# Four graph layers on one core: own features by a crossbar DMA, the last columns of v by matmuls, and the first chunk's adjacency rows loaded early

## The reference, cut to what matters

```python
h = relu(layernorm(x)); x = x + leaky_relu(A_norm @ [h[:2048] @ Wr; h[2048:] @ Wd] + bias)      # layer 0
h = relu(layernorm(x))                                                                          # layers 1 and 2
g = relu(concat([h, adj @ h], 1) @ W1);  x = x + relu(concat([g, adj @ g], 1) @ W2)
h = relu(layernorm(x)); x = x + relu((A_norm @ h) @ W.T + b)                                     # layer 3
h = relu(layernorm(x))                                                                          # attention
Wh1, Wh2 = (h @ W) @ a[:256], (h @ W) @ a[256:]
e = leaky_relu(Wh1 + Wh2.T, 0.2)
att, natt = softmax(where(adj > 0, e, -inf)), -softmax(where(adj > 0, -e, -inf))
x = x + elu(concat([att @ h, natt @ h], 1) @ wtrans)
```

## Time and profile before

| | us |
|---|---|
| median of 3 runs | 2246.96 (2246.89 to 2247.9) |
| the profiled execution, its own time | 2249.18 |
| its span, from the first to the last instruction | 2247.4 |
| PE busy | 2110.6 (94%) |
| ACT busy | 1473.8 (66%) |
| DVE busy | 1422.0 (63%) |
| mean granted TensorE clock | 0.98 of full |

### The profile page before, as it was taken

One profiled execution on the slowest core, in us unless ns is written; L12 is line 12 of the kernel. 1 busy time (PEld: TensorE's weight loads), 2 busy tenths in 40 slices (PEclk: granted clock), 3 DMA queues, 4 the chain that ended last, 5 costly groups with the idle time before them and its releaser, 6 DMA issues.

```text
span 2247.4 us, 27564 instructions
## 1 busy us (share of the span) xinstructions
PE 2110.6 (94%) x10932; PEld 1533.1 (68%) x10932; DVE 1422.0 (63%) x2335; ACT 1473.8 (66%) x1778; POOL 2.1 (0%) x12
## 2 busy tenths in 40 slices
PE   2678999999999999999998879999999999999998
PEld 2557888455554555554555358888888888888886
DVE  5667488100004332324445589999999999999774
ACT  5556666555547656556654457869686969787963
POOL 0000000000000000000000000000000000000000
PEclk9889999999999999999998989999999999999999
DMA  9989325100021101231117754626262627271300
GB/s 306 296 296 310 110 85 169 47 20 19 10 85 38 57 29 57 66 101 57 49 37 158 240 185 148 225 94 218 95 212 86 233 77 242 76 243 57 113 19 10
DMA packets 157647, 279.40 MB, mean 124 GB/s; under 512 B 10960, under 2 KB 83408, under 8 KB 149200
## 3 DMA queue, kind: packets, MB, share of 16 engines
q1 hardware_dynamic: 149072, 269.27, 36.5%
q10 hardware_dynamic: 8448, 8.39, 1.2%
HBM read 244.06 MB, written 33.57 MB: 124 GB/s over the span
## 4 chain that ended last, share of the span: by engine, by line
PE 81%; DVE 8%; DMA 6%; ACT 3%; issue 2%; SPq 0%; DVEq 0%; POOL 0%; ACTq 0%
PE ps L1604 39%; PE ps L1496 29%; PE ps L1521 6%; DMA work<-in_adj_t 5%; PE ps L1371 3%; ACT big L510 1%; PE ps L1467 1%; PE ps L1437 1%; DVE feat L1194 1%; PE ps L1424 1%; DMA t_spill<-acc 1%; DVE feat L1198 1%; DVE stat L1131 1%; DVE work L1130 1%; DVE work L1126 1%
## 5 line engine op out<-in xcount | busy, mean ns | idle before, releaser
L1496 PE MATMUL ps<-work,feat 128*128 128x512 bf16 x3072 | 671.3, 380 | 6.1 <-DVE feat L1068 4.3
L510 ACT ACTIVATE work<-big 128x1024 bf16<-128x1024 uint8 x460 | 481.4, 1053 | 244.3 <-PE ps L1496 222.0
L1496 PEld LDWEIGHTS ps<-work,feat 128*128 128x128 f16 x3072 | 300.1, 98 | 364.0 <-issue 6.8
L1604 PE MATMUL ps<-big,work 128*128 128x257 f32 x2048 | 452.0, 381 | 4.8 <-ACT work L808 4.8
L1604 PE MATMUL ps<-big 128*128 128x257 f32 x2048 | 449.4, 380 | 2.7 <-ACT big L808 2.7
L1604 PEld LDWEIGHTS ps<-big,work 128*128 128x128 f32 x2048 | 389.2, 191 | 61.0 <-issue 5.6
L1604 PEld LDWEIGHTS ps<-big 128*128 128x128 f32 x2048 | 388.3, 190 | 58.8 <-ACT big L808 3.5
L1371 PE MATMUL ps<-feat,work 128*128 128x256 f16 x2048 | 242.6, 280 | 13.7 <-DVE work L1002 7.1
L1371 PEld LDWEIGHTS ps<-feat,work 128*128 128x128 bf16 x2048 | 203.4, 100 | 51.0 <-DVE work L1002 11.7
L1100 DVE TENSOR_REDUCE gmax<-work 128x1 f32<-128x256 f32 x32 | 11.8, 414 | 261.9 <-ACT work L644 261.9
L808 ACT ACTIVATE work<-work 128x2048 f32<-128x2048 f32 x64 | 122.2, 1909 | 82.9 <-DVE work L1294 82.9
(11 more groups left out here) (158 smaller groups left out, 1562.4 us busy)
## 6 DMA issues: line engine op xcount, KB each, us to landing
work<-in_adj_t SPq DMA_DIRECT2D x128, 512.0 KB, 5.0
big<-in_adj_t SPq DMA_DIRECT2D x64, 1024.0 KB, 5.4
feat<-in_adj SPq DMA_DIRECT2D x58, 1024.0 KB, 7.3
h_spill<-work SPq DMA_DIRECT2D x32, 512.0 KB, 4.4
feat<-h_spill SPq DMA_DIRECT2D x32, 512.0 KB, 5.4
x_spill<-work SPq DMA_DIRECT2D x24, 512.0 KB, 3.0
work<-in_x SPq DMA_DIRECT2D x16, 512.0 KB, 5.5
work<-x_spill SPq DMA_DIRECT2D x16, 512.0 KB, 4.2
```

The lines of the kernel that those rows point to most:

```text
L510: return nc.scalar.activation(out_, in_, ACT.Copy, **kw)
L1496: ins = mm(ps[:, bank + f, :], parts[:, j, h, f * P:(f + 1) * P], stage[:, g % STAGES, jj, :], start=(fresh and h == 0), stop=(end and h = ...
L1604: ins = mm(ps[:, 4 * s + t, 0:YW], quads[k % RING][:, jj, t * P:(t + 1) * P], Yb[:, j, s, :], start=(j == 0), stop=(j == NT - 1), skip_gro ...
```

## The change

Three things change, with the waits and the orders that go with them.

1. **Own features by crossbar.** `own_features` (PE) and the first of the two evacuations per chunk (ACT) go. SP issues one transposing DMA per chunk of layers 1 and 2 (`transpose_own`, from `parts` to the new view `own`, in the space of `part3`), and DVE adds the two halves into `T_sb[:, 0:2]` (`add_own`, after the `post` of the chunk before). `project` also waits for `own_added`. There is one `own` buffer, so a transposing DMA waits until the chunk before it was added. The attention's weights are loaded to `part3` a layer later.
2. **v's last columns by matmuls.** Chunks 6 and 7 of v are no longer stored to DRAM and read back. PE spreads them (`spread_t`), ACT copies them to `t_row` (`t_copy`). The one load left from DRAM of chunks 2 and up covers four chunks.
3. **Rows early.** All 8 half rows of the first chunk have slots of their own: four over adjacency bytes that lie in Y's second half, four in the mask's space. The first four are loaded while layer 3's last chunk is still being summed. `y_copy(15)` and POOL's memset then wait for the first 8 searches, `mask_exponents(0, 0)` for 12. SP's order at the end of layer 3 is rewritten; reloads of chunks 4 and 5 come ahead of `store(6)`. PE's spread of the shift moves from behind projection 27 to behind projection 23, and ACT's copy of it likewise.

```diff
-    EVACS = [0, 2, 2, 1]
+    EVACS = [0, 1, 1, 1]
...
+                def transpose_own(c):
+                    if l == 1:
+                        sp.wait_ge(parts_in[c], 16)
+                    else:
+                        sp.wait_ge(split_done, NT + (c + 1) * TPC)
+                    wait(sp, own_added, (l - 1) * NC + c)
+                    sp.dma_start_transpose(own.rearrange("p t h k n -> p (t h k) n"),
+                                           parts[:, c * TPC:(c + 1) * TPC, :, :].rearrange("p j h f -> p (j h f)"))\
+                      .then_inc(own_in, 16)
+                if l in (1, 2):
+                    transpose_own(0)
+                    transpose_own(1)
                 for r in range(0, H - 1):
                     for s in range(2):
                         store(2 * r + s, s)
                         if l != 1:
                             refill(2 * r + s, s, r)
+                        if l in (1, 2):
+                            transpose_own(2 * r + s + 2)
...
+                else:                                  # l == 3
+                    for c in range(2):
+                        reload(l, c)
+                    sp.wait_ge(panel_ready, staged(3) + (NC - 1) * GROUPS + 8)
+                    for s in range(2):
+                        load_row0(s)
+                    reload(l, 2)
+                    for s in range(2, 4):
+                        load_row0(s)
+                    for c in range(3, 6):
+                        reload(l, c)
+                    store(NC - 2, 0)
+                    reload(l, NC - 2)
                     sp.wait_ge(panel_ready, staged(4))
                     sp.wait_ge(group_done, staged(4))
-                    sp.wait_ge(t_out, 16 * (NC - 1))
-                    load_t(2 * CH, 5 * CH, t_in)
+                    sp.wait_ge(t_out, 16 * (NC - 2))
+                    load_t(2 * CH, 4 * CH, t_in)
                     sp.wait_ge(out_ready, 3 * NT)
                     load_t(0, 2 * CH, t_in)
-                    sp.wait_ge(ht_ready, 4)
-                    for h in range(2):
-                        load_row(2, h)
-                store(NC - 1, 1)
+                    for s in range(4, 6):
+                        load_row0(s)
+                    store(NC - 1, 1)
+                if l in (1, 2):
+                    sp.wait_ge(own_added, l * NC)
+                reload(l, NC - 1)
                 if l == 3:
-                    spill_t(NC - 1)
-                    sp.wait_ge(t_out, 16 * NC)
-                    load_t(7 * CH, CH, t_last_in)
-                reload(l, NC - 1)
+                    for s in range(6, 8):
+                        load_row0(s)
...
+            def t_copy(n):
+                act.wait_ge(t_ps_ready, n + 1)
+                copy(t_row[:, (6 + n) * CH:(7 + n) * CH], ps[:, 4 - n, :]).then_inc(t_copied, 1)
...
+                def add_own(c):
+                    n = (l - 1) * NC + c
+                    dve.wait_ge(own_in, (n + 1) * 16)
+                    wait(dve, out_ready, n * TPC)
+                    nc.vector.tensor_tensor(T_sb[:, 0:FB, :].rearrange("p k (t n) -> p t k n", t=TPC),
+                                            own[:, :, 0, :, :], own[:, :, 1, :, :], ALU.add).then_inc(own_added, 1)
                 for c in range(NC):
                     post(c, c % 2, c // 2, ch)
+                    if l in (1, 2) and c + 1 < NC:
+                        add_own(c + 1)
...
-                        if g == TPC // PANELS - 1 and l in (1, 2):
-                            own_features(c)
...
+            def spread_t(c):
+                pe.wait_ge(t_col_ready, c + 1)
+                if c == NC - 1:
+                    pe.wait_ge(ht_evac, NC - 2)
+                for t in range(TPC):
+                    ins = spread(ps[:, 10 - c, t * P:(t + 1) * P], t_col[:, c * TPC + t:c * TPC + t + 1])
+                ins.then_inc(t_ps_ready, 1)
-            for c in range(1, EARLY):
+            transposed(1)
+            spread_t(NC - 2)
+            for c in range(2, EARLY):
                 transposed(c)
             pe.wait_ge(wt_in, 32)
-            for j in range(8):
+            pe.wait_ge(t_copied, 1)
+            for j in range(2):
+                projected(j)
+            spread_t(NC - 1)
+            for j in range(2, 8):
                 projected(j)
```

More of the change, by code:

```diff
@@ L390, in _ @@
                             refill(2 * r + s, s, r)
+                        if l in (1, 2):
+                            transpose_own(2 * r + s + 2)
                         if l == 3:
                             spill_t(2 * r + s)
[L393 to L400, removed]
+                if l < 3:
+                    for c in range(4):
+                        reload(l, c)
+                    store(NC - 2, 0)
+                    for c in range(4, NC - 1):
+                        reload(l, c)
+                    store(NC - 1, 1)
+                else:
+                    for c in range(2):
+                        reload(l, c)
+                    sp.wait_ge(panel_ready, staged(3) + (NC - 1) * GROUPS + 8)
[5 more added lines that the diff above has]
+                    for c in range(3, 6):
+                        reload(l, c)
+                    store(NC - 2, 0)
+                    reload(l, NC - 2)
@@ L615, in stage_groups, with evac @@
                              adj8[:, g * PANELS:(g + 1) * PANELS, bass.ts(c, CH)]).then_inc(panel_ready, 1)
-                def evac(c, e, s):
-                    if e == 0:
-                        wait(act, out_ready, c * TPC + (l - 1) * NT)
-                    if l in (1, 2) and e == 0:
-                        act.wait_ge(ht1_ready, c + (NC * (l - 1) + 1))
-                        bank = 4
-                    else:
-                        act.wait_ge(group_done, c * GROUPS + (staged(l) + GROUPS))
-                        bank = 2 * s
-                    copy(T_sb[:, 2 * e:2 * e + 2, :], ps[:, bank:bank + 2, :]).then_inc(evac_done, 1)
+                def evac(c, s):
+                    wait(act, out_ready, c * TPC + (l - 1) * NT)
+                    act.wait_ge(group_done, c * GROUPS + (staged(l) + GROUPS))
+                    k = 2 if l in (1, 2) else 0
+                    copy(T_sb[:, k:k + 2, :], ps[:, 2 * s:2 * s + 2, :]).then_inc(evac_done, 1)
                 def post_std(c):
@@ L719, in _ @@
                 if l == 3:
-                    for c in range(3):
+                    for c in range(2):
                         ht_copy(c)
+                    t_copy(0)
+                    ht_copy(2)
                 post_std(NC - 1)
@@ L832, in att_chunk @@
                         load_x3(c)
-            for j in range(8):
+            for j in range(2):
+                y_copy(j)
+            t_copy(1)
+            for j in range(2, 8):
                 y_copy(j)
@@ L1618, in _ @@
             transposed(NC - 1)
-            for j in range(16, 28):
+            for j in range(16, 24):
                 projected(j)
@@ L1628, in _ @@
             ins.then_inc(my_ps_ready, 1)
-            for j in range(28, NT):
+            for j in range(24, NT):
                 projected(j)
```

80 lines of the change are left out of this document (35 added, 45 removed).

## The result

The changed kernel takes 2209.5 us (median of 4 runs, 2203.5 to 2211.7) against 2246.9 us before (2246.5 to 2247.9): the ratio is 0.983, with a 95% interval of 0.981 to 0.985. The forecast was 2208.5 us and a ratio of 0.983.

What follows compares the result with a forecast made beforehand. PE bounds the kernel: its own work in layers 1 and 2 and its wait before attention. Span 2247.4 - 13.3 - 25.1 = 2209.0 us, median 0.4 less, 2208.5 us; range 2202 to 2222.

Steps and rivals of the forecast that it cites:

- First term: Layers 1 and 2: PE's 16 transposing matmuls per chunk go, 15 x 0.89 = 13.3 us less (bounds 12.5 and 14.2).
- there only the wait grows: Layer 1's first chunk: PE already stands 1.87 us for ACT after the matmuls, so this chunk is not counted as gain.
- Cover of the new work: Layers 1 and 2: DVE's addition (1.22 us) and the transposing DMA (5 to 21 us, about 33 free) cost 0.
- Second term: Start of attention, 1213 to 1342 us: PE runs unbroken from 1317.2 instead of 1342.32, 25.1 us less (22 to 27.5).
- PE and not DVE sets the next step: Before attention: PE's projections and spread end at 1272.5 us, DVE's `cc_ready` at 1271, so PE is later by 1.5 us.
- The stall at step 2: Attention's first steps: ACT has step 2's scores at 1297.2 us, DVE wants them at 1295.7; 1.5 us lost.
- Rival (a): Start of attention: slow DMA, or a wait for t_copy on ACT, delays the searches; 2213 to 2222 us, chance 0.17.
- (b): Layers 1 and 2: waiting for `add_own` or a slower copy takes 0.9 us per chunk, no gain; 2222 us, chance 0.06.
- (d): Start of attention: searches start early, but PE's 32 projections and low clock set the start; 2229 us, chance 0.04.
- Rival (c): Layers 1 and 2: a 42 us crossbar DMA, over 33 us free, paces every chunk; 129 us more, 2337 us, chance 0.05.
- The end: Attention after PE's unbroken run begins: each chunk costs PE the same, so moving that instant moves the end.

Runs made afterwards that it cites:

- rows_late: Changed kernel with SP's order and waits for rows and reloads as in the kernel before, eight slots and v by matmuls kept: 2209.1 us (one run).
- after_again: The changed kernel again, unchanged, timed and traced a second time: 2209.3 us (5 runs), ratio 0.983.
- cross_x7: Changed kernel with each chunk's transposing DMA issued seven times, each waiting for the one before: 2225.0 us (one run).
- cross_x9: Changed kernel with each chunk's transposing DMA issued nine times in a row: 2363.1 us (one run).
- extra_search: Changed kernel with two more searches on DVE, which nothing reads, behind the sixteen: 2210.6 us (4 runs), ratio 0.985.
- own_only: Kernel before with only the own features by crossbar added, attention's start as before: 2233.4 us (6 runs), ratio 0.994.
- own_undone: Changed kernel with own features back on PE, v's spread and early rows kept: 2218.1 us (5 runs), ratio 0.988.

## Why the prediction was right, and where it was not

- **First term, 13.3 us.** Right in mechanism; right in size (13.26 us) in the first trace and in rows_late's, which is partly luck, since 11.5 to 11.9 us, under its lower bound of 12.5, is what the four traces with the fall of the clock have. The step "there only the wait grows" is right in length (1.87 to 2.75 us) and incomplete in its result: in six of the eight traces with that pause, after_again's among them, the clock fell behind it, and 1.7 us went. The prediction gave no price for PE standing longer.
- **Cover of the new work.** The addition took 1.22 us, with 2.1 us to spare in layer 2's last chunk. The DMA took 4.3 to 7.3 us; the value "5 to 21 us" held its median, 5.1 us. cross_x7 and cross_x9 put the point from which it is paid between 32 and 40 us, with 33 forecast, and the cover of the first chunk at about 22 us. The Trainium skill, "VectorE: DVE Perf Modes", section on the three transpose paths, has 1309 ns for one block, an estimate of 20.9 us for 16 one by one; the trace does not agree, since the whole DMA landed in 7.3 us at the most. By "DMA: Bandwidth & Descriptors", section on latency and other measured facts, an estimate is 2 us (512 KB at 261 GB/s); no DMA here was faster than 4.3. Neither changed the sum.
- **Second term, 25.1 us; it was 26.5.** The searches start 17.5 us after P7 (18.1 forecast), sixteen without a gap. `cc_ready` follows at 56.8 us (57.6 forecast). That PE and not DVE sets the next step was right, by about 2 us (1.5 forecast; extra_search), of which 0.8 is the half clock behind P7. PE's row at 1304.42 comes 102.5 us after P7, 103.8 forecast. PE's spread starts 59.0 us after P7, forecast was 59.1. What the sum left out is part of the clock: from the spread to DVE's first step it has 5.3 us, and 3.6 was measured. It took 1 us off for the spread at the half clock (2.07 us in the earlier trace rows, 1.05 now), but not for the mean of Y behind it, 3.62 us before and 1.88 now. First before, then after:

```profile
1299.98 3.62 PE L1626 MATMUL ps<-part,hsum 128*128 128x512 f32 x4
```

```profile
1260.94 1.05 PE L1504 MATMUL ps<-ident,acc 128*128 128x128 f32 x8
1261.84 1.88 PE L1668 MATMUL ps<-part,hsum 128*128 128x512 f32 x4
```

- **The stall at step 2.** 1.5 us forecast, 1.32 measured, at the place and on the releaser named. The 0.49 us for a row of the adjacency on the next step was not foreseen: that load stands in SP's queue behind the load of a mask (L463), which is issued only when ACT has cast an earlier one (1285.6 us in the chain), and needs 7.4 us to land, so ACT's lateness is passed on through SP.
- **Rival (a), DMA too slow.** It did not come about. The prediction took 198 GB/s at a busy share of 1.00 as the rate of full engines, and that was too low. With the first rows moved ahead of chunk 2's reload the engines moved 399 GB/s from 1190 to 1200 us and 268 and 372 in the two windows behind. rows_late shows that the rival was real in another order: there the first search waits 6.9 us for v's load behind the rows. Two readings were off without effect: the store under way in the window of 118 GB/s is that of chunk 6, v's seventh, and of the reloads only those of chunks 4 and 5 were moved ahead.
- **Rivals (b) and (d)** did not come about either: there is no wait of PE for `add_own`. The clock, at 0.60 in the earlier trace rows, is 0.83 at the same place after P7 (the window from 1208.55 above), which cost 0.8 us and not the 20 of the rival. It is 1.00 in the window behind, in the projections:

```profile
1220.00:1230.00 10.00, 10.00 (x31) 4.96 (x30) 9.61 (x9) 3.59 (x6) 0.00 (x0) 1.00 0.78 286
```

- **Rival (c)** would have decided from where it was said to, at a higher price.
- **The end.** From the last row on nothing changed, 896.1 us in both, as the prediction assumed. The spread of the runs, 2203.5 to 2211.7, has the size of layer 0's variation, which no step of the prediction touched.

The experiments also tell the two parts of the second term apart: of 26.5 us, 20.5 go when v is stored and loaded again, and 7.0 when the rows are late again; together that is 1 us more than the whole, and the clock alone moves this stretch by about that much. Slots of their own for all eight half rows, and the earlier place of the spread of the shift, were not tested by themselves. What stays open is when the clock falls behind a pause and when not, and why the reload of chunk 4 landed 1.6 us sooner in own_only.

## What to carry to other kernels

A small piece of work on the engine that sets the end can be given to a slower path whose time lies under a whole period: count how many us are free until its result is wanted, also in the first and the last chunk, where it is less, and not how the two durations compare. When work is taken from the busiest engine, look where it had filled a pause, since a longer pause can cost clock behind it. And where the part of a kernel that no edit touches varies by more than the effect, cut the traces at the same instructions and compare the stretches: rows_late and the changed kernel have the same time and differ by 7 us.

## What the runs showed of the hardware

- A transposing DMA of 512 KB, SBUF to SBUF, landed in 4.3 to 7.3 us (16 in the kernel after), seven of them one after another in 30.2 to 33.3 us and nine in 38.9 to 42.7, so 4.3 to 4.8 us each. Its issue held SP's queue for 1.9 to 5.2 us, longer than that of a plain load (0.43 to 0.47 us for the two of the attention's weights, 256 KB each).
- At layer 1's start, a pause of 2.75 or 2.76 us of PE went with the half clock for about 3.4 us in six traces and with none in two, and a pause of 1.86 or 1.87 us with none in four. The same kernel showed both (after, after_again).
- In the window from 6.6 to 16.6 us after P7, with PE busy for 6.87 or 6.88 us, the clock was 0.83 in the kernel after and 1.00 in own_undone, cross_x7 and cross_x9.
- Layer 0, with the same instructions each time, ended between 381.0 and 391.2 us.
